# Float16 passes of split operands in the relation products of a graph kernel on one core

## What is computed

```python
x = x + _L0_gnn_ref(_layernorm(x), W, attn_src, attn_dst, edge_index, edge_type)
# in _L0_gnn_ref: r = 8 relations, h = 8 heads of d = 32
h_all = jnp.einsum('nf,rof->rno', x, W).reshape(r, n, h, d)
h_src = h_all[edge_type, src]
h_dst = h_all[edge_type, dst]
scores = einsum('ehd,hd->eh', h_src, attn_src) + einsum('ehd,hd->eh', h_dst, attn_dst)
# leaky relu, softmax over the edges of one dst, weighted sum of h_src
```

## Time and profile before

| | us |
|---|---|
| median of 3 runs (3273.65 to 3282.90) | 3278.91 |
| span of the profiled execution, first to last instruction | 2981.7 |
| median less span | 297.2 |
| first stage, to its last product | 430.6 |
| first instruction of `attend0` | 435.9 |
| TensorE busy in the span | 2202.5 (74%) |
| VectorE, ScalarE, GpSimd busy | 1825.0, 1348.8, 1568.8 |

### The profile page before, as it was taken

One profiled execution on the slowest core, in us unless ns is written; L12 is line 12 of the kernel. 1 busy time (PEld: TensorE's weight loads), 2 busy tenths in 40 slices (PEclk: granted clock), 3 DMA queues, 4 the chain that ended last, 5 costly groups with the idle time before them and its releaser, 6 DMA issues. The chain is left out here.

```text
span 2981.7 us, 48329 instructions
## 1 busy us (share of the span) xinstructions
PE 2202.5 (74%) x13240; PEld 1875.9 (63%) x13241; DVE 1825.0 (61%) x4491; ACT 1348.8 (45%) x3007; POOL 1568.8 (53%) x1492
## 2 busy tenths in 40 slices
PE   7999985776677767767665629672333499999998
PEld 6888874565565656556554617552331498999997
DVE  2321115777777777777757783376988666665665
ACT  3444445555556655555642205332340444444444
POOL 1137417777777777777752207456700255555554
PEclk8999996788877887887877559786555699999999
DMA  6455545555555554555594506674520522222331
GB/s 192 140 189 217 225 158 146 146 143 146 143 140 146 148 147 139 144 145 142 146 90 135 166 5 176 147 165 128 130 69 15 166 47 44 46 46 48 49 48 25
DMA packets 188405, 364.16 MB, mean 122 GB/s; under 512 B 44334, under 2 KB 120725, under 8 KB 181582
## 3 DMA queue, kind: packets, MB, share of 16 engines
q0 software_dynamic: 78160, 187.31, 28.2%
q1 hardware_dynamic: 106510, 171.10, 17.4%
q10 hardware_dynamic: 3584, 3.98, 0.5%
HBM read 247.26 MB, written 117.28 MB: 122 GB/s over the span
## 5 line engine op out<-in xcount | busy, mean ns | idle before, releaser
L785 POOL DMA_INDIRECT sum_ring<-h_tab,gnn_edge_row x880 | 839.4, 954 | 268.1 <-issue 256.6
L1047 PE MATMUL sum_bank<-sum_ring,sum_one_hot 128*128 128x264 f32 x1760 | 555.6, 473 | 140.6 <-issue 120.9
L1047 PEld LDWEIGHTS sum_bank<-sum_ring,sum_one_hot 128*128 128x128 f32 x1760 | 396.4, 236 | 235.3 <-issue 136.7
L699 PE MATMUL rows_bank<-rows_w_rows,rows_xnT 128*128 128x264 f32 x1568 | 361.4, 389 | 8.3 <-ACT rows_h_rows L495 8.3
L699 PEld LDWEIGHTS rows_bank<-rows_w_rows,rows_xnT 128*128 128x128 f32 x1568 | 296.5, 192 | 58.3 <-ACT rows_h_rows L495 9.1
L2110 POOL DMA_INDIRECT out_dram<-moe_y,slots_nodes x112 | 187.4, 1673 | 267.8 <-ACT moe_y L2133 250.7
L1036 PEld LDWEIGHTS sum_bank<-gnn_dst_half,sum_one_hot_T 128*128 128x128 f32 x1760 | 256.6, 224 | 28.5 <-issue 16.0
L831 ACT ACTIVATE sum_distance_by_lane<-all_iota,gnn_minus_local 128x128 bf16<-128x128 f32 x880 | 267.4, 386 | 0.1
L897 DVE TENSOR_TENSOR sum_ring<-sum_ring,sum_bank 128x1024 f32<-128x1024 f32 x220 | 264.2, 1211 | 0.7 <-ACT sum_ring L845 0.6
L1036 PE MATMUL sum_bank<-gnn_dst_half,sum_one_hot_T 128*128 x1760 | 247.2, 303 | 15.0 <-ACT sum_one_hot_T L824 11.8
L2101 POOL DMA_INDIRECT moe_tile<-normal,slots_rows x116 | 140.3, 1210 | 220.3 <-PEq L70 148.9
(11 more groups left out here) (436 smaller groups left out, 4538.2 us busy)
## 6 DMA issues: line engine op xcount, KB each, us to landing
h_tab<-rows_h_rows SPq DMA_DIRECT2D x49, 1056.0 KB, 4.0
sum_local_rows<-local_tab SPq DMA_DIRECT2D x110, 256.0 KB, 3.5
slots_stage<-in_L_ffn_W_dram SPq DMA_DIRECT2D x16, 1024.0 KB
sum_ring<-h_tab,gnn_edge_row POOLq DMA_INDIRECT x880, 3.1
mask_tab<-rows_masks POOLq DMA_DIRECT2D x7, 1560.0 KB
sum_masks<-mask_tab SPq DMA_DIRECT2D x28, 390.0 KB
results<-moe_tiles SPq DMA_DIRECT2D x80, 128.0 KB, 3.2
g_tab<-gnn_rows_out SPq DMA_DIRECT2D x49, 132.0 KB, 3.4
```

Of the source, the lines that this page charges most:

```text
L699: last = nc.tensor.matmul(bank[2 + r % 4][:, 0:W0], norm.xT[:, u, c * P:(c + 1) * P], wx[:, c, r, :], start=(c == 0), stop=(c == DC - 1))
L785: nc.gpsimd.indirect_dma_start(ring[:, t % (RING * ST), :], None, k.h_tab, bass.IndirectOffsetOnAxis(k.edge_row[:, t:t + 1], 0)).then_inc( ...
L1047: last = nc.tensor.matmul(sum_b[j][:, 0:W0], hot[:, m % 3, t, :], ring[:, m % RING * ST + t, :], start=(u == 0), stop=(u == G - 1))
```

## The change

The relation products and the destination product become one product over 2176 columns (8 x 264 + 64), in float16. Weights (times WS) and turned tiles (times XS) are split in a high half, the value rounded to float16, and a low half, the rest rounded to float16. Three passes, high by high, high weights by low rows, low weights by high rows, are summed in the same bank; ScalarE scales back when it copies. The 2176 columns are cut in five pieces (four of 436, one of 432), one for each of banks 2 to 6. The high halves are made by ScalarE (`keep`), the low ones by VectorE (`w_low`, `v_low`, `x_low`) from the same bank. The destination half is now copied by ScalarE from the last piece, and `half` is gone. The first x load goes ahead of the attention vectors, which all move to ScalarE's queue; `stored.start` becomes SyncE's first instruction; tile 0 is turned ahead of the attention products. The steps of the tables move to later tiles: `cuts` 3 to 4, `block_lines` 5 to 7, `groups` 7 to 9, `turn0` to `turn3` 9, 11, 13, 15 to 12, 14, 16, 18, the node store 16 to 19, the turning of tables (TURN0) 18 to 22, `first_edges` 26 to 32, `keep_first` 28 to 34, `turn5` 32 to 39, the gate store 36 to 43; `edge_rows`, `positions` and the statistics stay.

```diff
-        self.t_ps.done(act, t)
-        used.slot(act, t)
-        self.nc.scalar.activation(self.xT[:, u, :], self.banks[u][:, 0:D], ACT.Copy).then_inc(self.t_ok.sem, 1)
...
-        NF, TURN0 = E // P, 18
+        NF, TURN0 = E // P, 22
...
-        wx, wd = s.sb("w_rows", [P, DC, R, W0]), s.sb("w_dst", [P, DC, R * H0])
+        HW, CW = R * W0, R * W0 + R * H0
+        PW = 2 * (-(-CW // 10))
+        pieces = [(o, min(o + PW, CW)) for o in range(0, CW, PW)]
+        NP = len(pieces)
+        assert NP == 5 and pieces[-1][0] < HW and PW <= 512
+        wcat = [s.sb(f"w_{n}", [P, DC, CW], F16) for n in ("high", "low")]
+        xh = [s.sb(f"xnT_{n}", [P, 2, D], F16) for n in ("high", "low")]
...
-        h_ps, h_ok = Count(s, "h_in_psum", 4), Count(s, "h_kept", 4)
-        d_ps, d_ok = Count(s, "dst_half_in_psum", 2), Count(s, "dst_half_kept", 1)
+        h_ps, h_ok = Count(s, "h_in_psum", NP), Count(s, "h_kept", NP)
...
+        def w_turned(n, r):
+            return (wcat[n][:, :, r * W0:r * W0 + D], bank[2 + r % 4][:, :].rearrange("p (c o) -> p c o", c=DC))
+        def v_turned(n, i):
+            c, j = divmod(i, 2)
+            to = wcat[n][:, c, HW:CW].rearrange("p (r h) -> p r h", r=R) if j else wcat[n][:, c, 0:HW].rearrange("p (r w) -> p r w", r=R)[:, :, D:W0]
+            return to, bank[6][:, 0:DC * R * 2 * H0].rearrange("p (c r j h) -> p c r j h", c=DC, r=R, j=2)[:, c, :, j, :]
...
-            vectors(sp, 0, "L0_gnn_attn_src")
+            stored.start(sp)
             for j in range(2):
...
-                stored.start(sp)
                 for t in range(NT):
-                    sp.wait_ge(h_ok.sem, 8 * t + 8 + 4)
+                    sp.wait_ge(h_ok.sem, NP * t + NP + NP)
                     sp.dma_start(rows(k.h_tab.rearrange("(n r) o -> n (r o)", r=R), t * P, P), flat(hb[:, t % 2, :, :])).then_inc(stored.sems[t % 2], 16)
...
-                    if t == 8:
+                    if t == 10:
...
-                    if t == 10:
+                    if t == 12:
...
-                    if t == 4:
+                    if t == 5:
...
-                    if t == 16:
+                    if t == 19:
                         sp.wait_ge(node_ok, 1)
                         sp.dma_start(k.node_tab[1:1 + GC * P, :].rearrange("(c p) e -> p c e", p=P), node[:, :, :]).then_inc(node_st, 16)
...
-                    if t == 19:
+                    if t == 23:
                         sp.wait_ge(node_st, 48)
...
-                    if t == 36:
+                    if t == 43:
...
+            act.dma_start(k.x[:, 0:quarter[1], :], a["x"][0:quarter[1] * P, :].rearrange("(t p) f -> p t f", p=P)).then_inc(loaded[0], 16)
+            vectors(act, 0, "L0_gnn_attn_src")
             vectors(act, 1, "L0_gnn_attn_dst")
-            act.dma_start(k.x[:, 0:quarter[1], :], a["x"][0:quarter[1] * P, :].rearrange("(t p) f -> p t f", p=P)).then_inc(loaded[0], 16)
...
-            root(0)
-            norm.t_ok.start(act)
             h_ok.start(act)
-            norm.keep(act, 0, 0, d_ps)
+            for r in range(R):
+                if r == 4:
+                    root(0)
+                act.wait_ge(wt_ps, r + 1)
+                to, got_w = w_turned(0, r)
+                nc.scalar.activation(to, got_w, ACT.Copy, scale=WS).then_inc(wt_hi, 1)
+            def keep(t):
+                norm.t_ps.done(act, t)
+                if t >= 2:
+                    act.wait_ge(h_ps.sem, NP * t)
+                nc.scalar.activation(xh[0][:, t % 2, :], bank[t % 2][:, 0:D], ACT.Copy, scale=XS).then_inc(x_hi, 1)
+            keep(0)
+            act.wait_ge(v_ps, 1)
+            for i in range(4):
+                to, got_v = v_turned(0, i)
+                nc.scalar.activation(to, got_v, ACT.Copy, scale=WS).then_inc(v_hi, 1)
             for t in range(NT):
                 if t in (3, 10, 16):
                     root((3, 10, 16).index(t) + 1)
                 if t + 1 < NT:
-                    norm.keep(act, t + 1, (t + 1) % 2, d_ps)
+                    keep(t + 1)
                 stored.slot(act, t // 2, t % 2)
-                for r in range(R):
-                    h_ps.done(act, t * R + r)
-                    nc.scalar.activation(hb[:, t % 2, r, :], bank[2 + r % 4][:, 0:W0], ACT.Copy).then_inc(h_ok.sem, 1)
+                line_ = flat(hb[:, t % 2, :, :])
+                for q, (o0, o1) in enumerate(pieces):
+                    h_ps.done(act, t * NP + q)
+                    o1 = min(o1, HW)
+                    last = nc.scalar.activation(line_[:, o0:o1], bank[2 + q][:, 0:o1 - o0], ACT.Copy, scale=1.0 / (XS * WS))
+                    if q == NP - 1:
+                        last = nc.scalar.activation(k.dst_half[:, t, :], bank[2 + q][:, o1 - o0:o1 - o0 + R * H0], ACT.Copy, scale=1.0 / (XS * WS))
+                    last.then_inc(h_ok.sem, 1)
...
+            def w_low(r):
+                v.wait_ge(wt_hi, r + 1)
+                to, got_w = w_turned(1, r)
+                nc.vector.scalar_tensor_tensor(to, got_w, WS, w_turned(0, r)[0], ALU.mult, ALU.subtract).then_inc(wt_free, 1)
+            def v_low(i):
+                v.wait_ge(v_hi, 4)
+                to, got_v = v_turned(1, i)
+                nc.vector.scalar_tensor_tensor(to, got_v, WS, v_turned(0, i)[0], ALU.mult, ALU.subtract).then_inc(v_ok, 1)
+            def x_low(t):
+                v.wait_ge(x_hi, t + 1)
+                nc.vector.scalar_tensor_tensor(xh[1][:, t % 2, :], bank[t % 2][:, 0:D], XS, xh[0][:, t % 2, :], ALU.mult, ALU.subtract).then_inc(norm.t_ok.sem, 1)
...
+            norm.xn_ok.start(v)
+            norm.t_ok.start(v)
             stats(0)
             variance(0)
+            for r in range(4):
...
             scales(0)
-            norm.xn_ok.start(v)
-            d_ok.start(v)
-            def half(t):
-                d_ps.done(v, t)
-                nc.vector.tensor_copy(k.dst_half[:, t, :], bank[6][:, 0:R * H0]).then_inc(d_ok.sem, 1)
+            norm.normalise(v, 0, 0)
+            norm.normalise(v, 1, 1)
+            for r in range(4, R):
+                w_low(r)
+            x_low(0)
+            for i in range(4):
+                v_low(i)
...
-            turns_at = {1: edge_rows, 2: positions, 3: cuts, 5: block_lines, 7: groups, 9: turn0, 11: turn1, 13: turn2, 15: turn3, 26: first_edges, 28: keep_first, 32: turn5}
+            turns_at = {1: edge_rows, 2: positions, 4: cuts, 7: block_lines, 9: groups, 12: turn0, 14: turn1, 16: turn2, 18: turn3, 32: first_edges, 34: keep_first, 39: turn5}
...
-            norm.normalise(v, 0, 0)
-            norm.normalise(v, 1, 1)
             for t in range(NT):
+                if t + 1 < NT:
+                    x_low(t + 1)
                 if t + 2 < NT:
                     norm.normalise(v, t + 2, t % 2)
-                half(t)
...
+            norm.t_ps.start(pe)
+            h_ps.start(pe)
...
+            norm.transpose(pe, 0, 0)
...
+            passes = ((0, 0), (0, 1), (1, 0))
...
                 norm.t_ok.done(pe, t)
-                for r in range(R):
-                    h_ok.slot(pe, t * R + r)
-                    for c in range(DC):
-                        last = nc.tensor.matmul(bank[2 + r % 4][:, 0:W0], norm.xT[:, u, c * P:(c + 1) * P], wx[:, c, r, :],
-                                                start=(c == 0), stop=(c == DC - 1))
+                for q, (o0, o1) in enumerate(pieces):
+                    h_ok.slot(pe, t * NP + q)
+                    for n, (pw, px) in enumerate(passes):
+                        for c in range(DC):
+                            last = nc.tensor.matmul(bank[2 + q][:, 0:o1 - o0], xh[px][:, u, c * P:(c + 1) * P], wcat[pw][:, c, o0:o1],
+                                                    start=(n == 0 and c == 0), stop=(n == 2 and c == DC - 1))
                     last.then_inc(h_ps.sem, 1)
...
-                if t == 4:
+                if t == 5:
...
-                if t == 6:
+                if t == 8:
...
-                if t == 27:
+                if t == 33:
```

23 lines of the change are left out of this document (3 added, 20 removed).

## The result

The changed kernel takes 3174.36 us, the median of four runs (3163.43 to 3177.45). The kernel before, four runs beside it, takes 3276.28 (3269.51 to 3282.90). The ratio is 0.9681, with a 95% interval of 0.9657 to 0.9706: 102 us less, where 101 were forecast (3178); the interval alone is 96 to 112 us, so an agreement to 1 us is finer than the measurement. The profiled execution of the changed kernel took 3171.94 us by its own device time and has a span of 3170.2.

A forecast was written before the change was run, and what follows sets the result against it. TensorE bounds the first stage before; after, GpSimd's mask chain ends it: 326.3 + 7 + 1.3 = 334.6 us, against 327.4 by TensorE, so `attend0` begins 101 us earlier. 3278.9 - 101 = 3178 us, range 3160 to 3204.

The forecast's parts named there:

- The beat: Time from tile to tile in the first stage: 5.74 us, 2.00 us less, with 30 float16 matmuls a tile.
- The clock: TensorE's granted clock in the first stage, taken as 1.00 from tile 1 on.
- C: First stage: the clock swings, at 0.85 a tile takes 6.7 us, 47 us less gained, 3217 us; chance 0.07.
- D: First stage: waits keep the clock at 1.2 GHz, about 3440 us, slower than before; chance 0.03.
- The start: First loads and tile 0: first product at 27.7 us, tile 1's products at 36.5, 12.4 us earlier.
- The extras ahead of the node store: Waits between tile 1 and the node store, kept at 6.4 us, which put that store at 152.0 us.
- rival B: Table steps: waiting for gathers makes the node store 10 to 20 us late; 85 us gained, 3194 us; chance 0.18.
- rival E: Less waiting for the gathers and at the start than before: 115 us or more gained, 3162 us; chance 0.08.
- The mask chain: GpSimd's seven mask windows behind the node store: 174.3 us, plus 7 us from row stores sharing the transfer engines.
- The change of stage: From the last mask store's landing to the first instruction of `attend0`: 1.3 us, left of 5.2 without 3.9.
- Rival A: Mask chain doesn't slow down, or hides: TensorE and GpSimd end near 328 us; 108 us gained, 3171 us; chance 0.22.
- The first paragraph of the prediction: Whole kernel: span 2981.7 us, median 3278.9; the 297.2 us more taken as lying around the span, unchanged.

The follow-up runs named there:

- four_pass: Changed kernel with a fourth pass, low weights by low rows, added in every piece; 2971.28 us (one run).
- only_start: Kernel before with only the order of the first loads changed, products and steps as before; 2979.15 us, ratio 0.9971 to the kernel before.
- old_start: Changed kernel with the first loads in the order of the kernel before; 2894.88 us, ratio 0.9657 to the kernel before.
- aft_beside: Changed kernel, unedited, run again on another chip; 2889.36 us, ratio 0.9657 to the kernel before.
- aft_again: Changed kernel, unedited, run once more beside other variants; 2892.47 us, ratio 0.9683 to the kernel before.
- old_steps: Changed kernel with every table step back at its tile of the kernel before, arithmetic and start as changed; 2891.69 us.
- small_rows: Changed kernel storing 1/8 of each row from tile 20 on, rest filled later; whole time not meaningful, node store to last mask store 164.9 us instead of 171.4.
- last_mask_sp: Changed kernel with the seventh and last mask store issued on SyncE's queue instead of GpSimd's; 2886.58 us, ratio 0.9666 to the kernel before.
- mask_dve: Changed kernel with the seven mask windows computed on VectorE instead of GpSimd, which keeps loads and stores; 2885.05 us, ratio 0.9636 to the kernel before.
- one_pass: Changed kernel with only the first of its three passes, products with low halves left out; 2866.96 us (one run).
- base_look: Kernel before, nothing edited, run for a second trace; 2991.46 us with a span of 2989.7.

## Why the prediction was right, and where it was not

- **The beat** is right to 0.01 us, and with it the main claim. 48 x 2.01 us is 96 us of TensorE's path. Both prices, 0.417 ns a column and pass and 2.5 ns a matmul, carried over from the last stage, and `four_pass` shows that they hold for one more pass. ScalarE's copies were put at 0.54 and took 0.53; `x_low` at 0.45 and took 0.42.
- **The clock** stayed at 1.00 over 280 us with five banks in turn, so C and D did not happen. The price that D rests on is right, though its row gives it badly: 380 against 222.5 ns in the earlier trace rows is 1.7 times, while in the trace of after the pairs of tile 0 start 0.73 us apart at clock 0.50 and 0.37 at 1.00, which is double. The rule of the Trainium skill (TensorE: Matmul & The Clock Gate, "A second HAM failure mode: psum-queue depth-cycling"), weighed there against the trace of before, does not agree with this one either.
- **The start** was 0.6 us off, by two errors. The attention products, priced at 9.12 us by the earlier trace rows, took 11.09. In the trace of before the window 17.36 to 26.48 has a clock of 0.77; in that of after 16.6 to 27.8 has 0.63, and `only_start` shows the same 11.00. So the first product came at 29.56 instead of 27.7; from there to tile 1 it took 7.5 us, not the 8.8 between the two numbers of the text (its own terms, 5.74 and 2.7, make 8.4), which gave most of it back. The weights did come 3.4 us earlier (9.06 against 12.45), but 2.0 of it went into the slower attention products, and in `only_start`, where the root stands behind them, 0.3 is left. `only_start` and `old_start` show what counted: the slot wait with the float32 products, the earlier first product with the new ones.
- **The extras ahead of the node store** were kept at 6.4 us; they came to 2.6 (148.55 less 37.07 less 19 x 5.73). This is the step that failed by kind: the text held that nearly the same wait for the gathers would be met, with the next step late by 3 to 6 us. The gathers were issued from 91.46 to 101.2 us, and VectorE came to them only at 110.15 and did not wait (1.4 us in `aft_beside`, 1.6 in `aft_again`). Its timeline there:

```profile
104.80 5.31 DVE L531 BATCH_NORM_STATS2 nodes_stats<-nodes_acc 128x6 f32<-128x256 f32 x16
110.15 1.14 DVE L641 TENSOR_SCALAR rows_valid<-rows_lane,rows_of_group 128x256 f32<-128x256 f32 x4
```

  and in `aft_beside`:

```profile
109.14 1.14 DVE L641 TENSOR_SCALAR rows_valid<-rows_lane,rows_of_group 128x256 f32<-128x256 f32 x4 [1.43 <-DMA rows_group_dst<-dst_line,rows_edge_of_group]
```

  I counted tiles, 17.2 against 15.5 us, and forgot what stands in VectorE's queue of the new tile: `turn0` moved to tile 12, where statistics of the nodes, 5.31 us, stand ahead of it, and they now run while the gathers fly. From the end of `groups` VectorE reaches this wait after 16.8 us in `aft_beside` (90.9 to 107.7) and after 9.6 before (110.1 to 119.7): 5.3 of the 7.2 us are the statistics, 1.7 the tiles. TensorE's own extras fell too, from 10.2 to 4.5 us (316.6 less 37.07 less 48 x 5.73): from tile 1 on it waited 5.9 us before, most of it at these gathers, and 0.5 now. So its last product ended at 316.6 and not near 322. `old_steps`, with `turn0` at tile 9 and nothing ahead of it, waits 13.0 us. So rival B was wrong in sign, and the less waiting of rival E came true at this one place.
- **The mask chain** was put at 174.3 us to the end of its transfers and 7 of new contention. It took 171.3 to the last store's issue where it took 168.7, so 2.6 us more: the term was mis-sized. I let each window's wait hold as much of the row stores as 9 us of free transfer time would; `small_rows` shows that a window pays 0.9 us for them in all at this beat, so most of the row stores' transfer time costs the chain nothing. By the share of their rate (5.73 to 7.74) the closer beat should add 7.4 x (1 - 5.73/7.74) = 1.9 us (7.4 is 6.5 x 8/7, for whole stores), an estimate near the 2.6. But `four_pass` speaks against this account: its beat, 7.57 us, is nearly the old one, and its chain is as long as that of the changed kernel:

```profile
184.57 1.82 SPq L459 DMA_DIRECT2D node_tab<-rows_node  x1
...
356.20 0.84 POOL L411 DMA_DIRECT2D mask_tab<-rows_masks  x1 [0.30 <-POOL rows_masks L409]
```

  These are 171.6 us, with 45.0 us of waits for node rows, where the kernel before (both traces) takes 168.7 and 167.4 with 43.2 and 41.8. So the row stores cost the chain something, but what made it 2.6 us longer stays open; the single waits of the changed kernel run from 2.5 to 9.7 us, and how loads and row stores happen to meet may matter as much as the rate. The Trainium skill (DMA: Bandwidth & Descriptors, "Queues, rings and completion order"), by which queues share an engine in turn, fits the direction that `small_rows` shows; the size is small here.
- **The change of stage** was put at 1.3 us behind the last transfer; from the last slice with transfers (325.2) to 330.78 it took 5.6. I took it from a stage whose last store was SyncE's. `last_mask_sp` shows where the difference lies.
- These cancel: 3.4 us from the node store and 4.4 from contention against 4.3 for the change of stage, so `attend0` was 3.8 us ahead of the forecast of 334.6. That they cancel is luck: the sum was better than its terms.
- **Who sets the end.** As forecast, the mask chain, with TensorE done 14 us before the stage ends (316.6 against 330.8; the text had 334.6 less 322). Of these 14 us the change of stage behind TensorE's last product takes 5.8 (`mask_dve`), so TensorE had 8 to 9 us to spare. `mask_dve`, `one_pass` and `four_pass` show it from both sides. Rival A, both together near 328, did not happen.
- **The rest of the span shifts.** From the start of `attend0` to the next stage it takes 1165.5 us in `base_look` and 1167.6 in `aft_beside`: 2 us are given back of 104. The text's own sign, gathers one every 1.25 us and a stage of unchanged length, can't be read in the profile after: there it is one every 1.56 us (1376.5 us for 880), and no trace of the kernel before exists for that chip. `aft_beside` against `base_look` is what bears it out.
- **The first paragraph of the prediction was wrong**: "I take that part around the span as unchanged". There is no such part. The span of after, 3170.2, lies 1.7 us under its own time, and the 297.2 us are a difference between executions that `base_look` and the span of after put down to the chip. It did no harm, because the first stage is alike on both and the gain is a number of microseconds in that stage; as a ratio it is 0.968 where the kernel before takes 3276 us and 0.966 and 0.968 where it takes 2987, which the intervals don't tell apart. "The span would be 2881" is near on one kind of chip (2893.2 and 2886.3 measured) and 289 us off on the other.

## What to carry to other kernels

When a shortened engine gives way to a chain that is not touched, price that chain from its trigger, not from its share of the span, and find out what it costs when it is last: here it had 77 us to spare, all used up, and 10 us more of the stage lay in moving it to another engine. A wait of TensorE is dearer than its length when the clock is low behind it (5.8 us of waiting, 2.0 of clock in `old_steps`). When a step moves to another tile, read what else stands in its engine's queue at that tile; the distance in tiles is not the time. Before a span and a median are subtracted, see that they are of one chip.
